# Another order of the SBUF allocations in a four-layer kernel

## The reference

```python
x = L0_attn_x
xn = _layernorm(x); s = attention(xn, 16 heads of 128)
g = silu(mixture of 8 experts with routing, capacity and low-rank side paths, plus a shared ffn)
x = x + s * g
xn = _layernorm(x); s = one recurrent step (key, value, receptance, out products)
g = silu(linear(xn));                        x = x + s * g
xn = _layernorm(x); s = rotary attention;    g = silu(8 dense gated experts, all tokens)
x = x + s * g
xn = _layernorm(x); s = differential attention (16 maps)
g = silu(gated ffn 256 -> 1024 -> 256 with a Walsh-Hadamard transform inside)
x = x + s * g
```

## Time and profile before

| | |
|---|---|
| runs | 864.33, 865.74, 867.16 us; median 865.74 us |
| span of the profiled execution | 865.1 us, 15659 instructions |
| TensorE busy | 847.5 us, 98% of the span, 5436 matmuls |
| weight loads | 709.6 us, 82% |
| VectorE, ScalarE, GpSimd | 631.1 us (73%), 472.2 us (55%), 454.6 us (53%) |
| chain that ended last | TensorE 86% of the span |
| granted TensorE clock | 0.998 of full speed on the mean |

### The profile page before, as it was taken

How to read it: one execution, slowest core, us unless ns; L and a number is a source line. 1 busy time by engine, 2 the same in 40 slices (tenths; PEclk the granted TensorE clock), 3 DMA queues, 4 the chain that set the end, 5 groups by cost and what they waited for, 6 DMA issues and landing times.

```text
span 865.1 us, 15659 instructions
## 1 busy us (share of the span) xinstructions
PE 847.5 (98%) x5436; PEld 709.6 (82%) x5436; DVE 631.1 (73%) x1275; ACT 472.2 (55%) x944; POOL 454.6 (53%) x316
## 2 busy tenths in 40 slices
PE   8999999999999999999999999999999999999998
PEld 7888888888855899999998878878888887886688
DVE  6898989898987765664656869577667695345767
ACT  3666666666654565656643375732353335357743
POOL 6676767676623646565666021049808225708820
PEclk9999999999999999999999999999999999999999
DMA  8101010101006275456212150011111010030001
GB/s 328 42 19 36 18 36 18 36 18 36 1 1 258 98 241 187 169 169 210 75 42 88 50 206 1 1 50 43 43 36 36 13 62 1 1 146 3 3 2 49
DMA packets 23342, 62.17 MB, mean 72 GB/s; under 512 B 3136, under 2 KB 13632, under 8 KB 20224
## 3 DMA queue, kind: packets, MB, share of 16 engines
q1 hardware_dynamic: 21760, 57.35, 19.5%
q0 software_dynamic: 1536, 4.20, 1.5%
HBM read 50.00 MB, written 8.39 MB: 67 GB/s over the span
## 4 chain that ended last, share of the span: by engine, by line
PE 86%; DVE 7%; POOL 2%; ACT 2%; issue 1%; DMA 1%; SPq 0%; DVEq 0%; ACTq 0%; POOLq 0%
PE banks L102 26%; PE banks L104 25%; PE banks L103 25%; PE banks L1344 3%; PE banks L1330 1%; POOL arenaB L841 1%; DVE banks L1875 1%; POOL arenaC L841 1%; PE banks L999 1%; PE banks L1171 1%; PE banks L933 1%; PE banks L934 1%; DVE arenaC_rounded L1884 1%; PE banks L1013 1%; PE banks L854 1%
## 5 line engine op out<-in xcount | busy, mean ns | idle before, releaser
L2079 ACT ACTIVATE banks<-banks,small 128x512 f32<-128x512 f32 x128 | 84.9, 663 | 79.8 <-DVE small L1480 79.8
L1480 DVE TENSOR_REDUCE small<-banks 128x1 f32<-128x512 f32 x128 | 86.8, 678 | 10.6 <-PE banks L104 10.6
L102 PE MATMUL banks<-xnT_rounded,arenaD_rounded 128*128 128x512 f32 x224 | 89.4, 399 | 0.9 <-POOL arenaC_rounded L721 0.6
L104 PE MATMUL banks<-arenaC_rounded,arenaD_rounded 128*128 128x512 f32 (+1 forms) x256 | 89.6, 350 | 0.0
L103 PE MATMUL banks<-s_tok_rounded,arenaD_rounded 128*128 128x512 f32 x224 | 89.5, 400 | 0.0
L104 PE MATMUL banks<-xnT_rounded,arenaC_rounded 128*128 128x512 f32 x192 | 76.1, 396 | 0.0
L104 PE MATMUL banks<-xnT_rounded,arenaD_rounded 128*128 128x512 f32 x192 | 75.9, 395 | 0.0
L102 PE MATMUL banks<-arenaC_rounded 128*128 128x512 f32 (+1 forms) x192 | 71.4, 372 | 1.1 <-DVE arenaC_rounded L1633 0.6
L1495 DVE SCALAR_TENSOR_TENSOR arenaC<-banks,small,arenaC 128x512 f32<-128x512 f32 x96 | 71.2, 742 | 0.0
L103 PE MATMUL banks<-arenaD_rounded,arenaC_rounded 128*128 128x512 f32 (+1 forms) x192 | 68.5, 357 | 0.0
L707 POOL TENSOR_TENSOR arenaD_rounded<-arenaC,ones 128x512 fp32r<-128x512 f32 x30 | 31.2, 1040 | 55.3 <-DVE arenaC L1495 54.2
(11 more groups left out here) (431 smaller groups left out, 2725.7 us busy)
## 6 DMA issues: line engine op xcount, KB each, us to landing
arenaD<-in_wexp SPq DMA_DIRECT2D x8, 1060.0 KB, 6.3
arenaD<-in_wexp SPq DMA_DIRECT2D x8, 1024.0 KB, 4.8
arenaC<-in_wqkv SPq DMA_DIRECT2D x16, 384.0 KB, 3.1
arenaD<-in_wexp SPq DMA_DIRECT2D x8, 512.0 KB, 3.5
slots<-arenaB SPq DMA_DIRECT2D x1, 2560.0 KB, 10.5
arenaB<-in_sw SPq DMA_DIRECT2D x1, 2084.0 KB, 7.5
arenaC<-in_wo SPq DMA_DIRECT2D x1, 2048.0 KB, 15.9
arenaC<-slots SPq DMA_DIRECT2D x8, 256.0 KB, 3.2
```

The source lines that it names most:

```text
L102: pe.matmul(o, r(lhs[0]), r(rhs[0]), start=start, stop=False)
L104: return pe.matmul(o, r(lhs[1]), r(rhs[0]), start=False, stop=stop)
L1480: dve.tensor_reduce(negmax[:, n % 4:n % 4 + 1], bank[3 + n % 4][:, :], AX.X, ALU.max, negate=True).then_inc(max_done, 1)
L2079: act.activation(prob[r], prob[r], ACT.Exp, bias=negmax[:, r:r + 1], accum_out=rowsum[:, r:r + 1]).then_inc(exp_done, 1)
```

## The change

The tensors are allocated in another order. Nothing else differs: no instruction, no size, no offset inside an arena, no queue.

```diff
         g_tok = twinned("g_tok", [P, NT, D])
-        con = sb("con", [P, C_END])
         ones = sb("ones", [P, P])
         ones_r = sb("ones_r", [P, P])
+        arenaB = twinned("arenaB", [P, 16384])
+        arenaC = twinned("arenaC", [P, 12800])
+        small = twinned("small", [P, 1536])
+        arenaD = twinned("arenaD", [P, 2 * (WPACK + 2 * D)])
+        con = sb("con", [P, C_END])
         stats = sb("stats", [P, NT, 6])
         meanvar = sb("meanvar", [P, NT, 2])
         veps = sb("veps", [P, NT])
         rstd = sb("rstd", [P, NT])
         mhalf = sb("mhalf", [P, 256])
         ident = con[:, C_ID:C_ID + P]
-        arenaB = twinned("arenaB", [P, 16384])
-        arenaC = twinned("arenaC", [P, 12800])
-        arenaD = twinned("arenaD", [P, 2 * (WPACK + 2 * D)])
-        small = twinned("small", [P, 1536])
```

## The result

The changed kernel took 858.13 us (median; 856.68 to 858.83), the kernel before 866.45 us on the same chip: a ratio of 0.9912, 95% interval 0.9896 to 0.9928. Between the medians it is 8.3 us less; the ratio, which isn't that of the medians, stands for 7.6 us. The profiled execution spans 856.3 us instead of 865.1.

A forecast was written before the change was run, and what follows sets the result against it. TensorE was taken as the bound, its time being matmuls times their distance. Stage gains of 10.8 us less 1.5, 0.8 and 0.2 gave 8.3 us, so 865.7 − 8.3 = 857.4 us; range 854.9 to 867.0.

The forecast's parts named there:

- Attention of layer 0: In the heads of layer 0, 1020 matmuls come 5.9 ns closer each, 6.0 us gained, wholly on the path.
- `shared_hidden`: In this stage 108 matmuls go from 233.3 to 226.7 ns each, 0.7 us gained.
- `gate_up`: In the experts' `gate_up`, 384 matmuls gain up to 8.0 ns each, 3.1 us at most before deductions.
- settling: Every break of the stream costs 46 ns; 24 breaks in `gate_up` and some 8 elsewhere take 1.5 us off.
- stalls: At 16 stalls in `gate_up` TensorE waits for VectorE, so the saving of six matmuls ahead is idle: 0.8 us off.
- odd `down`: In `down` of the four odd experts, 192 matmuls go from 118.8 to 120.0 ns, a loss of 0.2 us.
- Gated ffn of layer 3: In the gated ffn of layer 3, 192 matmuls gain some 5.3 ns each, 1.0 us.
- `con` and its transposes: `con`, moving operand of some 230 transposes, goes from 0 to 64: 0 taken, bounds ±1.4 us.
- The step that failed: For all stages: operands at one place modulo 128 get the even 13.3 ns gap, 226.7 ns at 512 columns.
- Rival B: Uneven stages: place modulo 128 does not decide, they keep 232 to 235 ns, time 865.7 us; chance 0.26.
- The first rule that was weighed: Trainium skill on warm matmuls: columns over 2.4 GHz plus 2.5 ns, 215.8 ns at 512 columns anywhere; change worth nothing.
- plain float32 products: Said to agree with the skill's rule: 427 ns apart, two passes of 512 columns being 426.7, no gap to lose.

The follow-up runs named there:

- the first of these kernels: Computes nothing of the reference: rows of 60 one-pass products, start bytes of weights and moving operand or columns varied; at 512 columns both at 0 gave 226.8 ns.
- experiment 4: Computes nothing of the reference: rows of 60 products, weights 0 to 480 bytes off the moving operand; 512 columns: 232.3 ns at 128 off, 226.7 ns at 256.

## Why the prediction was right, and where it wasn't

The forecast was 857.4 us, by a gain of 8.3 us; measured were 858.13 us and 8.3 us. That the change acts through the places of the operands and the distance between matmuls is shown; that the size of the relation is 128 bytes was wrong, and the sum agrees partly by luck.

*Attention of layer 0*: 6.0 us forecast. The distance came down as forecast, to 226.6 ns. From the first to the last start of line 933 the stretch went from 215.3 to 209.9 us, 5.4 us less. Ahead of that another 0.5 us was gained and hidden. The first product of the first head starts later in this execution of the kernel after, and its column sum at 35.09 us against 35.15, so that the stretch between takes 24.8 us instead of 25.3 (timeline of TensorE, before, then after):

```profile
9.86 0.50 PE L102 MATMUL banks<-xnT_rounded,arenaD_rounded 128*128 128x512 f32 x1 [0.57 <-POOL arenaC_rounded L721]
```
```profile
10.30 0.50 PE L102 MATMUL banks<-xnT_rounded,arenaD_rounded 128*128 128x512 f32 x1 [1.01 <-POOL arenaC_rounded L721]
```

The later start belongs to the execution: the second ones of the two kernels begin at 10.10 and 9.67 us. The heads gave some 5.8 us in all, nearly the whole term.

*`shared_hidden`*: 0.7 us forecast. Its first half gave 0.4 (the lead from 5.4 to 5.8), the second some 0.3, of which 0.2 came back: at its end TensorE waits for VectorE (line 1671), 0.4 us in the kernel after against 0.2 before by the waits of TensorE. I had named such a return only for `gate_up`.

*`gate_up`*, net of settling, stalls and odd `down`: 3.1 − 1.1 (24 breaks at 46 ns) − 0.8 − 0.2 = 1.0 us forecast, 0.6 measured (7.6 to 8.2). *Gated ffn of layer 3*: 1.0 us less the breaks forecast, some 0.7 measured (8.2 to 8.9). The deductions were what kept the sum near: behind a stall the distance is still 233 ns for ten steps, and 3.1 us would have been five times too much.

*`con` and its transposes*: 0 forecast; they last 273 ns as before and cost no lead, right.

*The sum.* Of the 8.8 us between the two profiled executions, 1.7 are the late starts put down to issue in the kernel before, and 0.4 are missing through the later beginning of the kernel after. So the distances gave about 7.5 us where 8.3 was forecast: the heads came as costed, the other stages a little smaller. Counted in the same way, from the starts of the same matmuls less late starts, later beginning and clock, the other profiled executions with all of a head in agreement give 7.2 to 7.6 us. 7.5 us would be a ratio of 0.9913; the timed ones are 0.9912, 0.9899, 0.9934 and 0.9934, and 0.9948 with everything at 96. That the medians of the first timed pair lie 8.3 us apart, the forecast to the tenth, is luck.

*The step that failed* is the one that wrote "modulo 128" on all of it, as the change does. The rows ahead of the change could not separate 128 from 256, since the tensors in the even state there were in one relation. Rival B, "the place modulo 128 is not what decides", was literally right, and its time would have been the result had the new order happened to put the arenas 128 bytes off modulo 256, as the kernel with 32 bytes of padding had them: agreement modulo 128 in all but the weights of the column sums, and 0.9992 of the time. The new order puts them together modulo 512, which the forecast had not asked for and was saved by. I had weighed B at 0.26 by thinking of semaphores and changing tensors; the weakest point of the forecast was the size of the modulus, and it named no rival for that.

The first rule that was weighed is answered too. All steady distances of one-pass products of 512 columns here lie at 226.4 ns and above. The Trainium skill, "TensorE: Matmul & The Clock Gate", section "Back-to-back issue gap", would have 215.8 ns for 512 columns wherever they lie. That is its formula for an isolated matmul, which the prediction doesn't say; for a stream of weight loads and matmuls the section has about 131 ns, which nothing here comes near. The measurement decides, 226.4 to 234 ns by place. Nor do the plain float32 products agree with the formula, as the prediction has it: their 427 ns for two passes leave no 2.5 ns in either. What the Trainium skill's page "SBUF — State Buffer", section "Who interferes with whom", says of TensorE against other engines isn't contradicted: the kernels of rows of products had no other engine at work and show the same two distances.

## What to carry to other kernels

Where a kernel is bound by a dense stream of one-pass products with new weights each, read the distance between starts, not the duration; if wide products (512 columns here) settle in one stage and not in another, compare where weights and moving operands begin, modulo 256 bytes. A few floats of padding, or part offsets in multiples of 64 floats from starts at multiples of 32 bytes, cost nothing and gave 0.5 to 1% here; the stream needs stretches well over ten matmuls without a stall to have it. And before a sum is matched to a pair of traces, line up the starts of the same instruction in both: a fifth of this difference (1.7 of 8.8 us) lay in one place, and a second execution of the same kernel had another amount of it.

## What the runs showed of the hardware that was not expected

- The relation has a period of 256 bytes: w off by 32, 64, 96, 128, 160, 192, 224 gave 233.2, 233.3, 234.0, 232.3, 233.5, 229.0, 233.3 ns at 512 columns, and the same again within 0.2 ns from 256 on. Both at 16, 48 or 8 bytes gave 233.3, 233.2 and 232.8 ns although they agree. Why it is 256 bytes, and what happens inside TensorE or the memory, no run here shows.
- The settled gap above the columns depends on their number: about 13.3 ns at 512, 384, 320 and 256 columns, but 17.0 at 504, 16.7 at 496 and 480, 16.0 at 448 and 11.5 at 264. The next rows of the first of these kernels show two of them: 13.00 us / 60 − 200 ns for L99 (480 columns), 10.40 us / 60 − 160 ns for L101 (384). 128 columns take 110.8 ns, nearly what 256 take.

```profile
401.44 13.16 PE L99 MATMUL banks<-moving,weights 128*128 128x480 f32 x60
414.44 12.32 PE L100 MATMUL banks<-moving,weights 128*128 128x448 f32 x60
426.60 10.56 PE L101 MATMUL banks<-moving,weights 128*128 128x384 f32 x60
437.00 8.95 PE L102 MATMUL banks<-moving,weights 128*128 128x320 f32 x60
...
520.18 7.03 PE L112 MATMUL banks<-moving,weights 128*128 128x256 f32 x60
527.05 7.26 PE L113 MATMUL banks<-moving,weights 128*128 128x256 f32 x60
```

- At 256 columns one relation has two steady distances: w 64 bytes off settles at 6.87 us / 60 = 114.5 ns here (L112), and stays at 117.8 ns in the second kernel (L90, experiment 4), where it comes down to 113.5 ns when the moving operand also alternates between 0 and 256. What picks one of them stays open; it is 5% of a stage of narrow products.
